# Four layers with routed experts: halves of the hidden rows treated later in a step, and half-groups' weights loaded from ScalarE's queue

## The chip, the cores and the metric

One core of a Trainium2 chip. The metric is the device time of one execution in microseconds (us), as the median of several runs. The profile describes one further execution of the same program. Engines are named as in the profile: PE is TensorE (PEld its weight loads), DVE is VectorE, ACT is ScalarE, POOL is GpSimd, SP is SyncE (SPq its queue of DMA issues).

## The reference, cut to what matters

64 sequences of 64 tokens with 256 features pass through four residual layers. The stage that the change touches is layer 0:

```
rw = softmax(cond_8);  w, sel = top_k(rw, 2)          # two of 8 experts per sequence
out  = sum over the two chosen: w * (gelu(x @ gate) * (x @ up)) @ down     # 256 -> 1024 -> 256
out += the same with the shared expert's weights
x = x + out
```

Layers 1 (a weight matrix mixed per sequence), 2 (low rank) and 3 (one expert of 8, silu) follow and are not touched.

## The kernel before, in words

The kernel is written by hand, engine by engine. Each engine has its own list of instructions, and counting semaphores order them. Layer 0 first does the shared expert for half of the sequences, then the chosen experts, then the shared expert for the other half, interleaved with layers 1 and 2. The chosen stage has NR0 = 68 steps `s`. Sixty steps treat a full group: two sequences (128 token rows) that chose the same expert. Eight treat a mixed group in two halves, in which the two sequences have different experts. The steps stand as two first steps, a loop of NMIXED0 = 4 rounds of BODY = 16 steps `k` each, and two last steps. In a round the mixed half groups are the steps k = 4 (half 0) and k = 12 (half 1) (`HALVES`).

Products are done in split precision: fp32 data are split into a high part (by ACT) and a low part (by DVE). The 1024 hidden features of a group come in two halves, `h` = 0 and 1. In step s:

- PE does up and gate of half 0 of group s (L771 to L773, or L792 for a mixed group), then the down product of half 0 of group s-2 (L860 to L863), then up and gate of half 1 of group s, then down of half 1 of group s-2.
- ACT does `gelu` (L1298) of each half, the high part of the x of the next group (L1292), and the high parts `hh` of the turned hidden rows of group s-1 (`hidden_hi_chosen`, L1312, L1314).
- DVE does `hidden` (gelu times up, L1832), its transposition within squares of 32 (L1840), the low part of x (L1805), the low parts `hl` of the turned hidden rows of group s-1 (`hidden_lo_chosen`, L1845, L1847), and the weighted sum of group s-2 (`add`, L1909 to L1916).
- The other part of the transposition goes through DRAM: SP writes the squares (`write_square`, L422) and reads them back in turned order (`read_hidT`, L429). ACT's `hh` waits for this read, DVE's `hl` for `hh`, and the down product for `hl`.
- SP also loads the x of group s+2 (`load_skill`), stores finished rows (`store_chosen`, L376), and loads the mixed groups' expert weights (`load_mixed0`, L384): six pieces of 512 KB per half, that is gate, up and down for each of two experts.
- POOL loads the weights of the next expert in pieces of 512 KB on its own queue (L612) and splits them (L617, L619) in what is called a turn here; there is one turn per expert.

The order of DVE's work is written out in `chosen_group`: hidden 0, squares 0, x of the next group, `hl` 0 of s-1, hidden 1, squares 1, add of s-2, `hl` 1 of s-1. ACT's order is gelu 0, x, `hh` 0, gelu 1, `hh` 1. `hidT[h]` is one buffer per half, so that a read of it may start only when the low part of the group before has been made of it. In the kernel before that follows from DVE's order.

Of the kernel before, what the change touches and what calls it, by code (L numbers as in the profile page):

```python
# [40 lines left out]
E = 8  # L41
# [6 lines left out]
NR0 = FULL0 + 2 * NMIXED0  # L48
# [5 lines left out]
S0, S1 = EARLY, EARLY + NR0  # L54
# [8 lines left out]
PIECE = 1024  # L63
# [13 lines left out]
BODY = NR0 // NMIXED0 - 1  # L77
HALVES = (4, 12)
# [8 lines left out]
def place_at(m, k):  # L87

    m, k = m + k // BODY, k % BODY
    past = sum(k > at for at in HALVES)  # L90
    stored = 7 * m + 1 + k // 2 - (k > HALVES[0]) if k % 2 == 0 else 8 * m + 1 + k // 2
    return Place(2 + (BODY - 2) * m + k - past, HALVES.index(k) if k in HALVES else None, m, stored)


def place(s):

    return place_at((s - 2) // BODY, (s - 2) % BODY)
# [6 lines left out]
def build(nc, x, xT, cond, condT, w0, w1, mask, b1, w2, b2, w3, b3, out):  # L104
# [5 lines left out]
    with ExitStack() as ctx:  # L110
# [179 lines left out]
        def table_values(engine, at, top):  # L290

            return nc.values_load_multi_w_load_instructions(
                at, engines=[engine.engine], min_val=0, max_val=top,
                skip_runtime_bounds_check_because="the routing bounds what the table holds")[1]
# [15 lines left out]
        def _(sp):  # L310
# [62 lines left out]
            def store_chosen(g, r, at):  # L373
                sp.wait_ge(acc_done, g + 1)
                f = at.full if at.half is None else FULL0 + at.mixed
                sp.dma_start(chosen_rows[bass.ds(f, 1)].rearrange("a p d -> (a p) d"), chosen_out[r])\  # L376
                    .then_inc(stored[r], 16)

            def load_mixed0(m, half, pieces, free):
                experts = table_values(sp, chosen_mixed0[0:1, bass.ds(2 * m, 2)], E)  # L380
                sp.wait_ge(acc_done, free)
                for k in pieces:
                    i, e = k // 2, experts[k % 2]
                    sp.dma_start(mixed0_w[k], w0[bass.ds(e, 1), :, (3 * half + i) * PIECE:(3 * half + i + 1) * PIECE]  # L384
                                 .rearrange("a p n -> p (a n)")).then_inc(mixed0_in[i], 16)

            def load_chosen(n, u, buffer, after=None):

                slots = [s for i in range(4)
# [11 lines left out]
            for n in range(0, WPIECES - 4, 4):  # L401
                g = WFIRST + n // 2 + 4
# [15 lines left out]
            def write_square(s, p, h, at):  # L418

                n = P if at.half is None else S  # L420
                sp.wait_ge(squared, 2 * s + h + 1)
                sp.dma_start(squares[p, h].rearrange("p (g x) -> p g x", g=4)[:, :, 0:n],  # L422
                             square[h][:, 0:4 * n].rearrange("p (g x) -> p g x", g=4)).then_inc(square_out[h], 16)

            def read_hidT(s, p, h, at):

                n = P if at.half is None else S
                sp.wait_ge(square_out[h], 16 * s + 16)
                sp.dma_start(hidT[h].rearrange("p (a x) -> p a x", a=4)[:, :, 0:n],  # L429
                             squares[p, h].rearrange("(a i) (g x) -> (i g) a x", a=4, g=4)[:, :, 0:n])\  # L430
                    .then_inc(hidT_in[h], 16)
# [8 lines left out]
            write_square(1, 1, 0, FIRST_TWO[1])  # L440
            read_hidT(0, 0, 1, FIRST_TWO[0])
            write_square(1, 1, 1, FIRST_TWO[1])
            read_hidT(1, 1, 0, FIRST_TWO[1])
            with sp.Fori(0, NMIXED0) as m:
                for k in range(BODY):
                    s, p = 2 + BODY * m + k, k % 2
                    at, before = place_at(m, k), place_at(m, k - 1)
                    load_skill(S0 + s + 2, p, place_at(m, k + 2))
                    write_square(s, p, 0, at)
                    read_hidT(s - 1, 1 - p, 1, before)  # L450
                    if k < 2:
                        load_mixed0(m, 0, ((0, 1, 2, 3), (4, 5))[k], S0 + BODY * m)
                    if k in (HALVES[0] + 3, HALVES[0] + 4):
                        load_mixed0(m, 1, ((0, 1, 2, 3), (4, 5))[k - HALVES[0] - 3], S0 + BODY * m + HALVES[0] + 3)
                    write_square(s, p, 1, at)
                    read_hidT(s, p, 0, at)
                    if place_at(m, k - 2).half != 0:
                        store_chosen(S0 + s - 2, p, place_at(m, k - 2))

            def load_late(t, ks=(0, 1)):  # L460
                for k in ks:
                    sp.wait_ge(xl_done, S1 + 2 * t + k - 1)
                    load_x(EARLY + 2 * t + k, k)
# [8 lines left out]
            write_square(NR0 - 2, 0, 0, LAST_TWO[0])  # L472
            read_hidT(NR0 - 3, 1, 1, place(NR0 - 3))
            write_square(NR0 - 2, 0, 1, LAST_TWO[0])
            read_hidT(NR0 - 2, 0, 0, LAST_TWO[0])
            store_chosen(S1 - 4, 0, place(NR0 - 4))
            load_late(0, (1,))
            write_square(NR0 - 1, 1, 0, LAST_TWO[1])
            read_hidT(NR0 - 2, 0, 1, LAST_TWO[0])
            write_square(NR0 - 1, 1, 1, LAST_TWO[1])  # L480
            read_hidT(NR0 - 1, 1, 0, LAST_TWO[1])
            store_chosen(S1 - 3, 1, place(NR0 - 3))
            sp.wait_ge(hl_done, 2 * S1 - 2)
            read_hidT(NR0 - 1, 1, 1, LAST_TWO[1])
            load_late(1)
# [790 lines left out]
        def _(act):  # L1276
# [7 lines left out]
            def split_x(g, p, free=None, xset=1, mixed=False):  # L1284

                act.wait_ge(xraw_in[p], 16 * (g - p) + 32)
                if free is not None:
                    act.wait_ge(up_done, free)
                if mixed:
                    act.activation(xm[:, 0:P], xraw[p][:, 0:P], ACT.Copy).then_inc(xh_done, 1)  # L1290
                    return
                act.activation(xh[xset][p], xraw[p], ACT.Copy).then_inc(xh_done, 1)  # L1292
# [7 lines left out]
            def hidden_hi(h, n2, first=False):  # L1300
# [3 lines left out]
                    act.wait_ge(down_done, n2 - 1)  # L1304
                act.activation(hh[h], turn_ps[h][:, :], ACT.Copy).then_inc(hh_done, 1)

            def hidden_hi_chosen(s, h, at):

                act.wait_ge(hidT_in[h], 16 * s + 16)
                act.wait_ge(down_done, 2 * (S0 + s) + h - 1)  # L1310
                if at.half is None:
                    act.activation(by_chunk(hh[h]), turned_hid(h), ACT.Copy).then_inc(hh_done, 1)  # L1312
                else:
                    act.activation(hm[h][:, 0:P].rearrange("p (a t) -> p a t", a=4), turned_mixed(h, 0), ACT.Copy)\  # L1314
                        .then_inc(hh_done, 1)
# [44 lines left out]
                    hidden_hi_shared((q - 1) % 2, 2 * g + q - 1)  # L1360
                    mix(2 * q + 1)

            def chosen_group(s, p, at, before_at, after_at):

                g, n = S0 + s, 512 if at.half is None else D
                gelu(0, 2 * g, n=n)
                if before_at is None:
                    hidden_hi_shared(1, 2 * g - 1)
                if after_at is None:
                    for k in range(2):  # L1370
                        split_x(g + 1 + k, k, xset=0)
                else:
                    split_x(g + 1, 1 - p, free=2 * g, mixed=after_at.half is not None)
                if before_at is not None:
                    hidden_hi_chosen(s - 1, 0, before_at)
                gelu(1, 2 * g + 1, n=n)
                if before_at is not None:
                    hidden_hi_chosen(s - 1, 1, before_at)

            def group(g, p, n=3, after=1, xset=1):  # L1380
                gelu(0, 2 * g, first=n < 1)
# [33 lines left out]
            chosen_group(1, 1, FIRST_TWO[1], FIRST_TWO[0], place(2))  # L1415
            with act.Fori(0, NMIXED0) as m:
                for k in range(BODY):
                    chosen_group(2 + BODY * m + k, k % 2, place_at(m, k), place_at(m, k - 1), place_at(m, k + 1))
            chosen_group(NR0 - 2, 0, LAST_TWO[0], place(NR0 - 3), LAST_TWO[1])
            chosen_group(NR0 - 1, 1, LAST_TWO[1], LAST_TWO[0], None)  # L1420

# [174 lines left out]
        def _(dve):  # L1596
# [322 lines left out]
            def chosen_group(s, p, at, before_at, after_at, add_at=None):  # L1919

                g = S0 + s
                hidden_chosen(s, 0, at)
                if before_at is None:
                    hidden_lo_shared(1, 2 * g - 1)
                hidden_squares(s, 0, at)
                if after_at is None:
                    for k in range(2):
                        split_x(g + 1 + k, k, xset=0)
                else:
                    split_x(g + 1, 1 - p, mixed=after_at.half is not None)  # L1930
                if before_at is not None:
                    hidden_lo_chosen(s - 1, 0, before_at)
                hidden_chosen(s, 1, at)
                hidden_squares(s, 1, at)
                if before_at is None:
                    add_pair(g - 2)
                    return
                if add_at is not None:
                    add(g - 2, p, add_at)
                hidden_lo_chosen(s - 1, 1, before_at)  # L1940
# [317 lines left out]
```

## Time and profile before

| | us |
|---|---|
| median of 3 runs | 1205.19 |
| the three runs | 1205.19, 1205.22, 1196.62 |
| the profiled execution, its own time | 1200.89 |
| its span, first to last instruction | 1199.3 |
| PE busy in the span | 1134.5 |

A busy PE means that a matmul was in flight. The chosen stage lies between about 190 and 795 us of the span. The steps of one engine can be followed in the timeline, where a row is start, duration, engine, line and operation, with the idle time before it and its releaser in brackets.

### The profile page before, as it was taken

To read this page: it belongs to the slowest core of one execution; us is meant where nothing else is said; L and a number is where in the kernel's file an instruction comes from. 1 tells how busy PE (TensorE), PEld (TensorE's weight loads), DVE (VectorE), ACT (ScalarE), POOL (GpSimd) and SP (SyncE) were. 2 spreads that over 40 slices of the span, in tenths; PEclk is the share of its full clock that TensorE was granted. 3 is DMA by queue.
4 is the path that set the end of the run, shared out by engine and by line. 5 is a ranking of instruction groups with operands and counts; after the bars stand their busy time and mean duration, and the time that the engine had idled before them with its cause. 6 is when DMAs were issued, how large, how long until landed. Compare 5 with 4: busy or idle time off the path is not lost.

```text
span 1199.3 us, 25044 instructions
## 1 busy us (share of the span) xinstructions
PE 1134.5 (95%) x6894; PEld 956.9 (80%) x6895; DVE 743.0 (62%) x1255; ACT 428.2 (36%) x845; POOL 471.4 (39%) x296
## 2 busy tenths in 40 slices
PE   8999998998989999798997999989999999899998
PEld 7999996776776777676876677779999999678876
DVE  6775667657658587485875768655555555444443
ACT  5356532232222232222322232323332222566664
POOL 3278588106327045081451836010000000888840
PEclk9999999999999999899998999999999999999999
DMA  7189868777777866768667786556655546577753
GB/s 227 48 258 327 290 191 286 212 225 217 205 237 209 262 181 205 248 191 268 175 204 248 218 272 202 170 159 172 160 150 138 139 128 246 150 239 243 215 170 90
DMA packets 257126, 245.07 MB, mean 204 GB/s; under 512 B 89216, under 2 KB 216448, under 8 KB 254976
## 3 DMA queue, kind: packets, MB, share of 16 engines
q1 hardware_dynamic: 243344, 193.95, 53.4%
q0 software_dynamic: 13680, 49.81, 13.8%
q8 instruction: 57, 0.93, 0.3%
q14 instruction: 45, 0.37, 0.1%
HBM read 176.59 MB, written 67.11 MB: 203 GB/s over the span
## 4 chain that ended last, share of the span: by engine, by line
PE 70%; DMA 11%; DVE 7%; issue 5%; SPq 4%; ACT 2%; POOL 1%; DVEq 0%; ACTq 0%; POOLq 0%
PE bank L771 11%; PE bank L772 10%; PE bank L773 10%; DMA routing<-squares 10%; PE bank L1208 6%; PE bank L861 6%; PE bank L1237 3%; PE bank L792 3%; PE bank L1049 3%; PE bank L912 2%; PE bank L860 2%; PE bank L914 2%; PE bank L913 2%; PE bank L1186 2%; DVE FS L1832 1%
## 5 line engine op out<-in xcount | busy, mean ns | idle before, releaser
L617 POOL TENSOR_TENSOR W<-raw,one 128x1024 fp32r<-128x1024 f32 x79 | 150.8, 1909 | 565.9 <-DVE acc L1912 282.5
L861 PE MATMUL bank<-W,RS 128*128 x480 | 186.8, 411 | 34.4 <-DVE RS L1845 34.1
L771 PE MATMUL bank<-W,RS 128*128 (+1 forms) x512 | 206.9, 404 | 11.5 <-DVE RS L1805 9.1
L1845 DVE TENSOR_TENSOR RS<-routing,RS 128x512 fp32r<-128x512 f32 x120 | 130.4, 1087 | 131.3 <-ACT RS L1312 130.9
L1312 ACT ACTIVATE RS<-routing 128x512 fp32r<-128x512 f32 x120 | 75.8, 632 | 369.3 <-DMA routing<-squares 340.0
L619 POOL TENSOR_TENSOR W<-raw,W 128x1024 fp32r<-128x1024 f32 x79 | 200.2, 2535 | 6.2
L772 PE MATMUL bank<-W,RS 128*128 (+1 forms) x512 | 202.3, 395 | 0.0
L773 PE MATMUL bank<-W,RS 128*128 (+1 forms) x512 | 201.4, 393 | 0.0
L861 PEld LDWEIGHTS bank<-W,RS 128*128 128x128 f32 x480 | 91.8, 191 | 64.4 <-issue 49.7
L1298 ACT ACTIVATE FS<-bank 128x512 f32<-128x512 f32 (+1 forms) x200 | 114.2, 571 | 71.9 <-PE bank L773 70.2
L771 PE MATMUL bank<-RS,W 128*128 128x256 f32 x448 | 129.7, 289 | 1.0 <-DVE RS L1805 1.0
L771 PEld LDWEIGHTS bank<-W,RS 128*128 128x128 f32 x512 | 98.1, 192 | 40.4 <-issue 21.0
L773 PE MATMUL bank<-RS,W 128*128 128x256 f32 x448 | 127.0, 284 | 0.0
L772 PE MATMUL bank<-RS,W 128*128 128x256 f32 x448 | 127.0, 283 | 0.0
L773 PEld LDWEIGHTS bank<-W,RS 128*128 128x128 f32 x512 | 97.4, 190 | 21.2
L772 PEld LDWEIGHTS bank<-W,RS 128*128 128x128 f32 x512 | 97.9, 191 | 19.8
L1832 DVE TENSOR_TENSOR FS<-bank,FS 128x512 f32<-128x512 f32 (+1 forms) x136 | 88.7, 652 | 36.2 <-PE bank L773 27.3
L860 PE MATMUL bank<-W,RS 128*128 x360 | 102.9, 286 | 0.0
L771 PEld LDWEIGHTS bank<-RS,W 128*128 128x128 f32 x448 | 86.2, 192 | 1.3 <-issue 1.2
L772 PEld LDWEIGHTS bank<-RS,W 128*128 128x128 f32 x448 | 86.2, 192 | 0.1
L773 PEld LDWEIGHTS bank<-RS,W 128*128 128x128 f32 x448 | 86.1, 192 | 0.0
L1208 PE MATMUL bank<-W,RS 128*128 x336 | 84.0, 399 | 0.4 <-issue 0.3
(236 smaller groups left out, 2046.9 us busy)
## 6 DMA issues: line engine op xcount, KB each, us to landing
raw<-in_w POOLq DMA_DIRECT2D x87, 512.0 KB, 4.9
acc<-in_w SPq DMA_DIRECT2D x70, 512.0 KB, 5.5
routing<-squares SPq DMA_DIRECT2D x120, 256.0 KB, 3.2
mixes<-acc SPq DMA_DIRECT2D x16, 1024.0 KB, 6.2
W<-mixes SPq DMA_DIRECT2D x16, 1024.0 KB, 6.1
squares<-X SPq DMA_DIRECT2D x60, 256.0 KB, 2.4
squares<-acc SPq DMA_DIRECT2D x60, 256.0 KB, 2.9
FS<-in_xT SPq DMA_DIRECT2D x200, 64.0 KB, 2.9
```

What stands on the lines that cost most here:

```text
L617: pool.tensor_tensor(hi, raw[:, k, :], ones_like(PIECE), ALU.mult).then_inc(done, 1)
L619: pool.tensor_tensor(lo, raw[:, k, :], hi.bitcast(F32), ALU.subtract).then_inc(done, 1)
L771: pe.matmul(ps, ah, bh, start=(i == 0), stop=False)
L772: pe.matmul(ps, ah, bl, start=False, stop=False)
L773: mm = pe.matmul(ps, al, bh, start=False, stop=(i == n - 1))
L860: pe.matmul(ps, chunk(hl[h], c), w2_[:, 0, :], start=False, stop=False)
L861: mm = pe.matmul(both, chunk(hh[h], c), w2_, start=(h == 0 and c == 0), stop=(h == 1 and c == 3))
L1208: mm = pe.matmul(ps[:, :], chunk(x, c), w, start=False, stop=(c == 1 and x is x3l), skip_group_check=True)
L1298: act.activation(gl[h][:, 0:n], gate_ps[h][:, 0:n], ACT.Gelu_apprx_tanh).then_inc(gelu_done, 1)
L1312: act.activation(by_chunk(hh[h]), turned_hid(h), ACT.Copy).then_inc(hh_done, 1)
L1832: TT(hid[h][:, 0:n], up_ps[h][:, 0:n], gl[h][:, 0:n], ALU.mult).then_inc(hid_done, 1)
L1845: TT(by_chunk(hl[h]), turned_hid(h), by_chunk(hh[h].bitcast(F32)), ALU.subtract).then_inc(hl_done, 1)
```

## The change

1. DVE: `hl` 0 of group s-1 moves behind hidden 1 and squares 1 of group s, and stands ahead of the add of s-2. In a step whose add belongs to a mixed half 0 it stands between hidden 1 and squares 1.
2. ACT: gelu 1 moves ahead of `hh` 0. The order is gelu 0, x, gelu 1, `hh` 0, `hh` 1.
3. SP: `read_hidT(s, 0)` moves behind `store_chosen(s-2)`. That store waits until the add of group s-2 is done, and this wait now also protects `hidT[0]`. In the first steps a wait for `hl` is added, and in the last two steps the stores move likewise.
4. `load_mixed0` moves from SP to ACT, behind gelu 1, and its pieces are spread. Half 0 has pieces 0 and 1 at k = 0, and pieces 2, 3, 4, 5 at k = 1, 2, 3, 4. Half 1 has the same at k = 7 and k = 8 to 11. Before, there were four pieces at k = 0 (7) and two at k = 1 (8).

```diff
@@ SP
-            def load_mixed0(m, half, pieces, free):
-                ...
             write_square(1, 1, 1, FIRST_TWO[1])
+            sp.wait_ge(hl_done, 2 * S0 + 1)
             read_hidT(1, 1, 0, FIRST_TWO[1])
             with sp.Fori(0, NMIXED0) as m:
                 for k in range(BODY):
...
                     read_hidT(s - 1, 1 - p, 1, before)
-                    if k < 2:
-                        load_mixed0(m, 0, ((0, 1, 2, 3), (4, 5))[k], S0 + BODY * m)
-                    if k in (HALVES[0] + 3, HALVES[0] + 4):
-                        load_mixed0(m, 1, ((0, 1, 2, 3), (4, 5))[k - HALVES[0] - 3], S0 + BODY * m + HALVES[0] + 3)
                     write_square(s, p, 1, at)
-                    read_hidT(s, p, 0, at)
                     if place_at(m, k - 2).half != 0:
                         store_chosen(S0 + s - 2, p, place_at(m, k - 2))
+                    read_hidT(s, p, 0, at)
@@ ACT
+            def load_mixed0(m, half, pieces, free):
+                experts = table_values(act, chosen_mixed0[0:1, bass.ds(2 * m, 2)], E)
+                act.wait_ge(acc_done, free)
+                for k in pieces:
+                    i, e = k // 2, experts[k % 2]
+                    act.dma_start(mixed0_w[k], ...).then_inc(mixed0_in[i], 16)
...
+                gelu(1, 2 * g + 1, n=n)
+                if mixed is not None:
+                    m, k = mixed
+                    if k <= HALVES[0]:
+                        load_mixed0(m, 0, ((0, 1), (2,), (3,), (4,), (5,))[k], S0 + BODY * m)
+                    elif HALVES[0] + 3 <= k < HALVES[0] + 8:
+                        load_mixed0(m, 1, ((0, 1), (2,), (3,), (4,), (5,))[k - HALVES[0] - 3],
+                                    S0 + BODY * m + HALVES[0] + 3)
                 if before_at is not None:
-                    hidden_hi_chosen(s - 1, 0, before_at)
-                gelu(1, 2 * g + 1, n=n)
-                if before_at is not None:
-                    hidden_hi_chosen(s - 1, 1, before_at)
+                    for h in range(2):
+                        hidden_hi_chosen(s - 1, h, before_at)
@@ DVE
-                if before_at is not None:
+                hidden_chosen(s, 1, at)
+                first = add_at is not None and add_at.half == 0
+                if first:
                     hidden_lo_chosen(s - 1, 0, before_at)
-                hidden_chosen(s, 1, at)
                 hidden_squares(s, 1, at)
...
+                if not first:
+                    hidden_lo_chosen(s - 1, 0, before_at)
                 if add_at is not None:
                     add(g - 2, p, add_at)
                 hidden_lo_chosen(s - 1, 1, before_at)
```

## Rows read from the trace of the kernel before

**Rows 1.** The page: busy time of each engine in the span.
```profile
PE 1134.5 (95%) x6894; PEld 956.9 (80%) x6895; DVE 743.0 (62%) x1255; ACT 428.2 (36%) x845; POOL 471.4 (39%) x296
```

**Rows 2.** PE's waits between 200 and 800 us: total, times, longest.
```profile
PE bank L861 <- DVE RS L1845: 33.7, 18, 5.9
PE bank L771 <- DVE RS L1805: 9.1, 8, 1.7
```

**Rows 3.** Timeline of PE, SP, ACT, 480 to 503 us, around one set of pieces.
```profile
480.07 0.39 PE L771 MATMUL bank<-W,RS 128*128 x1
...
480.85 1.90 SPq L384 DMA_DIRECT2D acc<-in_w  x4
...
483.98 0.49 PE L861 MATMUL bank<-W,RS 128*128 x1 [1.03 <-DVE RS L1845]
...
485.90 0.49 PE L771 MATMUL bank<-W,RS 128*128 x1 [0.25 <-issue]
...
492.98 0.63 ACT L1312 ACTIVATE RS<-routing 128x512 fp32r<-128x512 f32 x1 [9.17 <-DMA routing<-squares]
...
494.75 0.79 PE L861 MATMUL bank<-W,RS 128*128 x1 [5.85 <-DVE RS L1845]
...
497.47 0.63 PE L771 MATMUL bank<-W,RS 128*128 x1
...
502.89 0.40 PE L771 MATMUL bank<-W,RS 128*128 x1
```

**Rows 4.** The chain that ended last, 470 to 500 us: start, duration, what.
```profile
479.80 0.80 SPq L292
...
483.67 9.29 DMA routing<-squares
```

**Rows 5.** Windows: length, busy of PE, PEld, DVE, ACT, POOL, clock, DMA share, GB/s.
```profile
471.00:480.00 9.00, 9.00 (x46) 7.59 (x45) 6.22 (x12) 2.54 (x5) 0.00 (x0) 1.00 0.53 161
480.00:490.00 10.00, 7.62 (x34) 5.50 (x32) 2.31 (x4) 1.42 (x3) 0.00 (x0) 1.00 0.92 296
490.00:500.00 10.00, 5.25 (x14) 4.33 (x15) 5.08 (x9) 2.81 (x6) 0.00 (x0) 0.66 0.83 263
...
585.00:620.00 35.00, 34.34 (x180) 25.75 (x178) 29.29 (x35) 9.32 (x20) 29.93 (x18) 1.00 0.71 203
```

**Rows 6.** PE's timeline: first and last of the 18 stalls near sets of pieces.
```profile
200.47 0.49 PE L861 MATMUL bank<-W,RS 128*128 x1 [1.41 <-DVE RS L1845]
...
724.46 0.49 PE L771 MATMUL bank<-W,RS 128*128 x1 [1.05 <-DVE RS L1805]
```

**Rows 7.** Timeline of a step without pieces or turn, 422 to 431 us.
```profile
423.33 0.68 DVE L1832 TENSOR_TENSOR FS<-bank,FS 128x512 f32<-128x512 f32 x1
...
425.15 0.39 PE L861 MATMUL bank<-W,RS 128*128 x1
...
425.89 0.69 DVE L1845 TENSOR_TENSOR RS<-routing,RS 128x512 fp32r<-128x512 f32 x1 [0.73 <-ACT RS L1312]
...
426.08 0.43 SPq L429 DMA_DIRECT2D routing<-squares  x1
426.50 0.68 DVE L1832 TENSOR_TENSOR FS<-bank,FS 128x512 f32<-128x512 f32 x1
...
427.21 0.71 DVE L1840 STREAM_TRANSPOSE acc<-FS 128x512 f32<-128x512 f32 x1
...
429.28 0.39 PE L861 MATMUL bank<-W,RS 128*128 x1
...
429.83 0.69 DVE L1845 TENSOR_TENSOR RS<-routing,RS 128x512 fp32r<-128x512 f32 x1 [0.92 <-ACT RS L1312]
```

**Rows 8.** Timeline in a turn of POOL, 442 to 448 us.
```profile
442.88 0.54 SPq L429 DMA_DIRECT2D routing<-squares  x1
...
444.08 2.60 DVE L1845 TENSOR_TENSOR RS<-routing,RS 128x512 fp32r<-128x512 f32 x1 [0.92 <-ACT RS L1312]
...
447.01 0.31 ACT L1314 ACTIVATE acc<-routing 128x128 f32<-128x128 f32 x1 [2.17 <-DMA routing<-squares]
```

More of the change, by code:

```diff
@@ L377, in store_chosen @@
                     .then_inc(stored[r], 16)
-            def load_mixed0(m, half, pieces, free):
[L380 to L385, printed above, removed]
             def load_chosen(n, u, buffer, after=None):
@@ L474, in _ @@
             write_square(NR0 - 2, 0, 1, LAST_TWO[0])
+            load_late(0, (1,))
+            store_chosen(S1 - 4, 0, place(NR0 - 4))
             read_hidT(NR0 - 2, 0, 0, LAST_TWO[0])
-            store_chosen(S1 - 4, 0, place(NR0 - 4))
-            load_late(0, (1,))
             write_square(NR0 - 1, 1, 0, LAST_TWO[1])
@@ L480, in _ @@
             write_square(NR0 - 1, 1, 1, LAST_TWO[1])
+            store_chosen(S1 - 3, 1, place(NR0 - 3))
             read_hidT(NR0 - 1, 1, 0, LAST_TWO[1])
-            store_chosen(S1 - 3, 1, place(NR0 - 3))
             sp.wait_ge(hl_done, 2 * S1 - 2)
@@ L1305, in hidden_hi @@
                 act.activation(hh[h], turn_ps[h][:, :], ACT.Copy).then_inc(hh_done, 1)
+            def load_mixed0(m, half, pieces, free):
[3 more added lines that the diff above has]
+                    i, e = k // 2, experts[k % 2]
+                    act.dma_start(mixed0_w[k], w0[bass.ds(e, 1), :, (3 * half + i) * PIECE:(3 * half + i + 1) * PIECE]
+                                 .rearrange("a p n -> p (a n)")).then_inc(mixed0_in[i], 16)
             def hidden_hi_chosen(s, h, at):
@@ L1361, in pair_shared, with chosen_group @@
                     mix(2 * q + 1)
-            def chosen_group(s, p, at, before_at, after_at):
+            def chosen_group(s, p, at, before_at, after_at, mixed=None):
                 g, n = S0 + s, 512 if at.half is None else D
@@ L1417, in _ @@
                 for k in range(BODY):
-                    chosen_group(2 + BODY * m + k, k % 2, place_at(m, k), place_at(m, k - 1), place_at(m, k + 1))
+                    chosen_group(2 + BODY * m + k, k % 2, place_at(m, k), place_at(m, k - 1), place_at(m, k + 1),
+                                 (m, k))
             chosen_group(NR0 - 2, 0, LAST_TWO[0], place(NR0 - 3), LAST_TWO[1])
```

## The prediction

> **What bounds the kernel now.** I read the page first. PE is busy for 1134.5 of 1199.3 us [rows 1], so the core is nearly matmul-bound, and the most that can be won by better ordering is what PE loses. Then I read PE's waits in the chosen stage. They come to 33.7 us for the low part of the turned hidden rows, 9.1 us for the low part of x [rows 2], and about 2 us of small ones: 44.8 us together. The question is what makes `hl` late. A clean step shows that it need not be: up-and-down units on PE follow each other every 4.13 us (425.15 to 429.28, [rows 7]), so a full step takes 8.26 us, with no idle time.
>
> The timeline around a set of pieces shows the cause [rows 3, 4]. Four pieces of 512 KB are issued at 480.85 on SP's queue. The read of turned rows issued behind them at 483.67 lands only after 9.29 us. In the clean step the same read takes 3.1 us (issued 426.08, landed when ACT's `hh`, 0.63 us before `hl` at 429.83, could start [rows 7]). ACT waits 9.17 us, gelu 1 stands behind that wait, DVE waits for `hh`, and PE stops for 5.85 us. The same set had already stopped PE for 1.03 us at 483.98 and 0.25 us at 485.90. There are eight such sets (two halves in each of four rounds).
>
> Idle time is not the whole loss. The starts of up and gate at 480.07, 485.90, 497.47 and 502.89 are 5.83, 11.57 and 5.42 us apart against 4.13, which is 1.70 + 7.44 + 1.29 = 10.4 us lost for 7.13 us idle, a factor of 1.46. Part of the difference is matmuls that run slower behind the stop: the mean granted clock of 490 to 500 us is 0.66 [rows 5], so for part of that stretch TensorE had its lower level of 1.2 GHz. PE had been idle for 5.85 us before.
>
> I went through PE's timeline for the stalls within some 20 us behind a set. There are 18, the first at 200.47 and the last at 724.46 [rows 6], with 32.6 us idle: 5.3, 1.1, 3.9, 1.8, 7.1, 3.2, 7.2 and 3.1 us for the eight sets. Times 1.46 they cost 47.7 us. The other 12.2 us idle (some 18 us of loss) lie in turns of POOL, in which DVE's operations are stretched: an `hl` takes 2.60 us in place of 0.69 [rows 7, 8].
>
> **The change part by part.**
>
> *Pieces on ACT's queue, one per step.* What it removes from SP is 1.90 us of issue at k = 0 and the 0.80 us of register loads ahead of it [rows 3, 4]. What matters more is the burst. Four pieces delayed one read by 9.29 - 3.1 = 6.2 us, that is 1.5 us per piece (the other two pieces of the set, issued later, has no part in this). The critical loop in a step is hidden 0, squares 0, write, read, `hh` 1, `hl` 1, hidden 0 of the next step. It took 7.11 us in the clean step (423.33 to 430.44, where `hl` of 429.83 ends [rows 7]), against 8.26 us that PE needs, so it regains 1.15 us per step. If a piece still costs a read 1.5 us, a step with one piece has a loop of 8.6 us, 0.4 us too long, and the step with two has 10.2 us, 1.9 us too long. A set then builds up 1.9 + 4 x 0.4 = 3.5 us of lag. `hl` 1 has 2.9 us in hand (done 430.52, wanted 4.13 us behind 429.28, at 433.41), so 0.6 us of it reaches PE. Sets that fall into a turn of POOL have less in hand. I take 1.5 us per set, 12 us in all. The bounds are 0 and the whole lag with nothing in hand, 28 us.
>
> The trace shows no DMA issue and no such register load on ACT in this stage. By SP's rows a load costs 0.80 us and an issue about 0.48 us. That is 1.8 us of ACT at the step with two pieces and 1.3 us at the others, between gelu 1 and `hh` 0. It delays `hh` 0 and `hh` 1. ACT is busy 2.54 of 9 us in a clean stretch [rows 5], and `hh` 0 is now wanted only behind squares 1, so I take 0. The upper bound is that all of it reaches PE: 8 x (1.8 + 4 x 1.3) = 56 us. The lower bound is 0. The wait for the add count in front of the pieces asks for an add made a step earlier and is met. Behind it on ACT stand `hh` 0 and 1, and behind those DVE's `hl` and the down product. POOL's own loads keep their place on their own queue.
>
> *gelu 1 ahead of `hh` 0.* In the clean step `hh` 0 came from the read and delayed gelu 1, so that hidden 1 started at 426.50 though its matmuls had ended about 425.3. DVE waited 0.73 us there [rows 7]. The edit frees this time, and a late read of half 0 no longer holds up hidden 1 and the next write. On a clean step this is worth nothing, since PE doesn't wait. In turns of POOL it gives up to 0.73 us in each of about 30 steps (a turn is some 35 us [rows 5], 4.2 steps, seven or eight turns), an upper bound of 20 us.
>
> *`hl` 0 behind squares 1.* This is what the change costs. With time counted from the start of the down product of half 1 in step s (425.15 in the clean step), hidden 1 can start at about +0.25, squares 1 ends at +1.64, and `hl` 0 at +2.35. The down product of half 0 wants it at +4.13 [rows 7], less some 0.4 us between the end of `hl` and the start of PE (`hh` of 0.63 us from 492.98 and `hl` of 0.69 us end at 494.3, PE starts at 494.75 [rows 3]). So 1.3 us are in hand, where before `hl` 0 ended at 426.58, with 2.7 - 0.4 = 2.3 us in hand. In a clean step that costs nothing. Where POOL holds `hl` 0 for 2.60 us [rows 8], it ends 0.6 us too late. Over 30 steps that would be 18 us, if each were hit in full. DVE is busy 29.29 of 35 us in such a turn, against 6.22 of 9 us outside [rows 5]. That is 0.84 against 0.69, or 1.2 us more per step over five operations that can be hit, so a typical step isn't hit in full. I take 5 us lost here and 2 us won by the gelu edit: net 3 us. The bounds are 18 lost and 20 won.
>
> *The read of half 0 behind the store.* It is now issued after the add of s-2, which needs two operations behind `hl` 0: about +3.4, and the store and its own issue bring it to +4.0, against +3.3 before. It lands at +7.1, and `hh` 0 ends at +7.8. It is wanted at 8.26 + 1.64 = +9.9. Nothing is late until a read takes over 5 us. Price 0. SP's x load behind it moves by the same 0.7 us at most, and is not wanted for another step. The added wait at the start and the moved stores at the end count once each, 0 to 1.4 us, taken as 0.
>
> *The sum.* -47.7 + 12 + 3 = -33 us, against the profiled execution's own 1200.89 us: 1168 us. The median of the runs is 4.3 us above that execution, and the lowest run is 4.3 us below it, so I leave the forecast there: **1168 us**, a gain of some 3%. A part of the gain may be lost outside the stage, though I see no row for it: PE is the bound behind it too.
>
> **The rivals.**
>
> *The queue makes no difference.* In the trace the read is late by what lies in front of it, and the share of the DMA engines rises from 0.53 to 0.92 when a set runs [rows 5]. If bytes alone count and nothing is in hand at most sets, each set costs its whole lag of 3.5 us, 28 us in all. The time is then 1201 - 47.7 + 28 = **1181 us**, or 1184 with the 3 us above. For it speaks that some sets fall into turns, where a read already takes 4.1 us (442.88 to 447.01 [rows 8]). Against it speaks that the share has room: a clean step has 0.53, and one piece a step adds little over 0.1. The Trainium skill (DMA: Bandwidth & Descriptors, Issuing engines are not separate DMA queues) states this as a rule: DMAs of several issuing engines share the same 16 engines, and another issuer saves only issue time. By that rule this rival would hold, and the gain would come from the spreading alone. The same page (Queues, rings and completion order) has each DMA engine take turns between the queues' rings, packet by packet, by which a short read would pass a long piece of another queue; the trace has no case on the hardware queues to tell.
>
> *DVE gains too.* The stalls in turns shrink as well, since DVE no longer waits in mid-step: 18 us of loss fall by half, and the pieces cost only the 0.6 us of an undisturbed set, 5 us in all. Then 1201 - 47.7 + 5 - 9 = **1149 us**. For it speaks the 0.73 us wait in each step; against it the smaller reserve of `hl` 0.
>
> *`hl` 0 is late in most steps: slower.* The place is DVE's `hl` 0 behind squares 1, and behind it the add, the store and the read of the next group. It decides from the point at which a read of half 0 takes longer than 5.0 + 1.3 = 6.3 us in a step without a turn, or 4.4 us in one where POOL stretches `hl` 0 by 1.9 us. Reads take 3.1 us clean and 4.1 us in a turn. With a piece beside it, at 1.5 us, a read in a turn takes 5.6 us and is over. If some 55 of 68 steps have a turn or a piece and lose 1.5 us each, that is 82 us: 1201 - 47.7 + 82 = **1235 us**. Against it speaks that pieces and turns seldom meet, and that 3.1 + 1.5 = 4.6 us is under 6.3.
>
> *Nothing moves.* The stalls come from DVE's order and not from the reads, or new ones take their place one for one: about 1200 us. The 9.29 us in the chain [rows 4] speak against it.
>
> **How the numbers follow.** Chances: forecast (1158 to 1176) 0.52, queue rival (1176 to 1189) 0.18, DVE gains 0.14, nothing 0.07, slower 0.09. The range should leave out the slower case and the "nothing" case: 1147 to 1191. It holds the bound of 28 us for the pieces plus several us of the `hl` bound, and nearly the whole case of DVE's gain on the other side. About 12 us (1%) is what a measurement of this kernel can tell from no change. Faster by over 1%: 0.52 + 0.18 + 0.14 = 0.84, less 0.02 for the queue rival's tail: 0.82. Within 1%: 0.07 + 0.02 and a share of the mild end of the slower case: 0.10. Slower: 0.08.
>
> **What the profile after should show.** PE's wait for L1845 falls from 33.7 us to 5 to 15 us, with no single stall above 3 us near the pieces. The reads behind a piece land within 5 us. ACT's longest wait for a read falls from 9.2 to some 5 us. A third DMA queue appears with the 48 pieces. In a clean step gelu 1 runs right behind its matmuls, and DVE has `hl` 0, add and `hl` 1 in a row, with a wait only before the last. The stalls in turns remain, some by the new place of `hl` 0. The granted clock no longer dips in windows like 490 to 500 us. The prediction is wrong if the reads take 6 us or more beside single pieces, if ACT's register loads take several us, or if DVE's order makes PE wait in clean steps.

## The result, and the profile after

The changed kernel takes 1193.32 us (median of 20 runs, 1186.63 to 1199.33), the kernel before 1202.26 us (median of 20 runs, 1196.62 to 1206.87). The ratio is 0.9928, with a 95% interval of 0.9907 to 0.9949. That is a gain of 0.7% or some 9 us, where 33 us were forecast. The profiled execution took 1193.86 us, its span is 1192.3 us.

PE's waits in the chosen stage, 200 to 800 us (line, releaser: total, times, longest), which answer to [rows 2]:

```profile
PE bank L850 <- DVE RS L1849: 22.4, 20, 1.9
PE bank L760 <- DVE RS L1809: 7.9, 8, 1.4
PE bank L760 <- DVE FS L1836: 7.0, 6, 1.5
```

The long stops are gone: the longest wait for the low part of the hidden rows is 1.9 us, against 5.9 us. But the total of the stage is still some 40 us against 44.8 us. Many short stops have come in place of few long ones, and PE now also waits for hidden 0 (L1836).

The page's queues, and the transposition's DMAs with their medians (count, size, us to landing):

```profile
q1 hardware_dynamic: 236432, 168.78, 46.8%
...
q10 hardware_dynamic: 6912, 25.17, 7.2%
...
routing<-squares SPq DMA_DIRECT2D x120, 256.0 KB, 3.9
...
squares<-X SPq DMA_DIRECT2D x60, 256.0 KB, 3.3
squares<-acc SPq DMA_DIRECT2D x60, 256.0 KB, 4.0
```

q10 is ACT's queue with the 48 pieces (25 MB). In the kernel before, the page has 3.2, 2.4 and 2.9 us for the three last rows. All three are now longer in the median over the whole execution.

The timeline of a step with one piece, outside POOL's turns, which answers to [rows 3] and [rows 7]:

```profile
413.53 0.34 ACTq L1301 DMA_DIRECT2D acc<-in_w  x1
...
413.95 0.33 SPq L414 DMA_DIRECT2D squares<-X  x1
...
414.32 0.43 SPq L421 DMA_DIRECT2D routing<-squares  x1
...
415.63 0.65 DVE L1849 TENSOR_TENSOR RS<-routing,RS 128x512 fp32r<-128x512 f32 x1
...
416.20 0.47 DVE L1916 TENSOR_SCALAR acc<-bank,weight 128x256 f32<-128x256 f32 x1
...
417.47 0.35 SPq L376 DMA_DIRECT2D chosen_rows<-acc  x1
...
419.69 0.38 SPq L421 DMA_DIRECT2D routing<-squares  x1
...
420.45 0.63 ACT L1309 ACTIVATE RS<-routing 128x512 fp32r<-128x512 f32 x1 [5.75 <-DMA routing<-squares]
```

Two things are to be seen. The piece is issued at 413.53, just ahead of the write of half 0 (413.95) and the read of half 1 (414.32). That read lands only when ACT can start at 420.45, 6.1 us later, against 3.1 us in [rows 7]. The read of half 0 could have gone at 417.82, behind the store, but goes at 419.69: it waits for the write of 413.95, which took about 5.7 us. So a piece holds up both halves of the round trip. DVE meanwhile does what the change asks: `hl` 0 at 415.63 right behind squares 1, then the add.

The windows which answer to [rows 5] (length, busy of PE, PEld, DVE, ACT, POOL, clock, DMA share, GB/s):

```profile
396.00:432.00 36.00, 35.58 (x171) 29.27 (x170) 21.89 (x40) 11.00 (x22) 0.00 (x0) 1.00 0.76 222
480.00:490.00 10.00, 8.60 (x41) 6.72 (x40) 5.08 (x9) 2.43 (x5) 0.00 (x0) 1.00 0.80 248
```

The DMA share is 0.76 over a whole set, where before it stood at 0.92 behind a burst and at 0.53 without. In these windows the granted clock is full. It still dips once in the stage, in a turn of POOL (here a window of 10 us with the same columns):

```profile
650.00:660.00 10.00, 7.48 (x35) 5.10 (x34) 7.79 (x8) 2.11 (x5) 8.88 (x6) 0.76 0.93 268
```

Before, there were five such dips (near 210, 350, 493, 562 and 643 us). Over the span the clock is 0.994 against 0.989.

The idle time of PE has also moved. I count as a turn each stretch in which POOL's splits follow each other, and 2 us behind it. Between 195 and 785 us PE idled 20.7 us in turns and 24.0 us outside them in the kernel before. Now it idles 32.6 us in turns and 8.0 us outside.

### The profile page after: what moved, and what is told of

Same layout as the page of the kernel before. It is cut to its first block, busy times and chain, and to the rows that moved or that the text cites. A ratio compares the mean times of both kernels' runs of the same rounds, so it can differ in the third digit from the quotient of the medians.

```text
span 1192.3 us, 25071 instructions
## 1 busy us (share of the span) xinstructions
PE 1130.8 (95%) x6894; PEld 951.8 (80%) x6895; DVE 743.8 (62%) x1255; ACT 430.0 (36%) x845; POOL 468.0 (39%) x296
## 4 chain that ended last, share of the span: by engine, by line
PE 60%; DMA 16%; DVE 8%; issue 7%; SPq 5%; ACT 2%; POOL 1%; ACTq 1%; DVEq 0%; POOLq 0%
DMA routing<-squares 14%; PE bank L760 10%; PE bank L761 9%; PE bank L762 9%; PE bank L1197 7%; PE bank L1226 3%; PE bank L850 3%; PE bank L1038 2%; DVE FS L1836 2%; PE bank L901 2%; DVE RS L1809 2%; PE bank L1175 2%; PE bank L903 2%; PE bank L902 2%; DVE X L1844 1%
## 5 line engine op out<-in xcount | busy, mean ns | idle before, releaser
L850 PE MATMUL bank<-W,RS 128*128 x480 | 183.5, 404 | 23.4 <-DVE RS L1849 22.9
L761 PE MATMUL bank<-W,RS 128*128 (+1 forms) x512 | 200.9, 392 | 0.0
L608 POOL TENSOR_TENSOR W<-raw,W 128x1024 fp32r<-128x1024 f32 x79 | 196.9, 2492 | 6.2
L760 PEld LDWEIGHTS bank<-W,RS 128*128 128x128 f32 x512 | 96.7, 189 | 50.8 <-issue 30.8
L850 PEld LDWEIGHTS bank<-W,RS 128*128 128x128 f32 x480 | 90.4, 188 | 52.7 <-issue 38.7
L761 PE MATMUL bank<-RS,W 128*128 128x256 f32 x448 | 127.1, 284 | 0.0
L1836 DVE TENSOR_TENSOR FS<-bank,FS 128x512 f32<-128x512 f32 (+1 forms) x136 | 88.6, 652 | 47.7 <-ACT FS L1287 32.7
L762 PEld LDWEIGHTS bank<-W,RS 128*128 128x128 f32 x512 | 96.6, 189 | 20.5
L761 PEld LDWEIGHTS bank<-W,RS 128*128 128x128 f32 x512 | 96.7, 189 | 18.8
L849 PE MATMUL bank<-W,RS 128*128 x360 | 101.7, 282 | 0.0
L761 PEld LDWEIGHTS bank<-RS,W 128*128 128x128 f32 x448 | 86.3, 193 | 0.1
L1197 PE MATMUL bank<-W,RS 128*128 x336 | 84.1, 399 | 0.4 <-issue 0.3
```

The source lines that it names most:

```text
L608: pool.tensor_tensor(lo, raw[:, k, :], hi.bitcast(F32), ALU.subtract).then_inc(done, 1)
L760: pe.matmul(ps, ah, bh, start=(i == 0), stop=False)
L761: pe.matmul(ps, ah, bl, start=False, stop=False)
L762: mm = pe.matmul(ps, al, bh, start=False, stop=(i == n - 1))
L849: pe.matmul(ps, chunk(hl[h], c), w2_[:, 0, :], start=False, stop=False)
L850: mm = pe.matmul(both, chunk(hh[h], c), w2_, start=(h == 0 and c == 0), stop=(h == 1 and c == 3))
```

## The experiments

All ratios are to the kernel before, run on the same chip (medians of 1199.6 to 1203.1 us there). In all of them the layout of the work is as told above; only what is named is changed.

**The two parts of the change, each alone.** First the pieces on ACT's queue in the old order:

```diff
  ACT:  gelu 0, x, hh 0, gelu 1,
+       load_mixed0 (the change's schedule),
        hh 1
  SP:  -load_mixed0;   DVE and the reads as before
```

> The order of before on all engines; only the loading of the mixed groups' pieces moves to ACT's queue, one per step (two in the first). Theory N (neighbours): a piece on a queue of its own slows every write and read of squares beside it by about 3 us, as the read issued at 414.32 in the changed kernel took 6.1 us and the write at 413.95 5.7 us; it does so in 40 steps, where the burst did it in 16. Then this kernel shows most of what the change won and lost: 1185 to 1200 us, with ratio 0.985 to 1.00, reads of 5 to 6 us beside pieces. Theory O (order): the burst was worth the 33 us forecast and hl 0 behind squares 1 gave 24 us back in POOL's turns. Then this kernel is the fastest, some 1165 to 1175 us, ratio 0.97 to 0.975.

Measured: 1195.96 us, 0.991 (0.987 to 0.995). This is the changed kernel's own gain. Theory O falls here: the order gave nothing back.

Then the order alone, with the bursts on SP's queue:

```diff
  the changed kernel's DVE, ACT and SP order
-       ACT: load_mixed0, spread
+       SP:  load_mixed0, pieces 0 to 3 at k = 0 (7), 4 and 5 at k = 1 (8)
```

> The new order on DVE, ACT and SP, with the pieces in bursts of four and two on SP's queue as before. Theory N: the stalls behind the bursts stay, a little smaller because gelu 1 and hidden 1 no longer wait for the late read: 1190 to 1203 us. Theory O: the bursts cost as before and the smaller reserve of hl 0 comes on top: 1212 to 1230 us, ratio 1.01 to 1.02, PE waits for the low part of the hidden rows in POOL's turns at the mixed groups.

Measured: 1205.98 us, 1.0024 (1.0006 to 1.0043), 3 us above theory N's range of 1190 to 1203 us and 6 us below theory O's. With a burst in front, the new order doesn't help.

**The same spreading on SP's queue.**

```diff
  the changed kernel
-       ACT, behind gelu 1: load_mixed0, spread
+       SP, between read_hidT(s - 1, 1) and write_square(s, 1): load_mixed0, same schedule
```

> As the changed kernel, but the pieces, one per step as there, are issued by SP behind the read of half 1. This tells the queue from the spreading. If the queue matters by letting short reads pass (the ring rule of the notes), this is slower than the changed kernel by some 10 us: about 1203 us. If a queue of its own is what hurts, because write and read ahead of a piece are now slowed by it too, this is faster: 1175 to 1185 us. If only bytes count (another issuer saves only issue time), it is equal within 4 us: 1190 to 1197 us.

Measured: 1181.26 us, 0.9821 (0.9786 to 0.9856). It is faster than the changed kernel by 12 us, with intervals apart. The same pieces in the same steps cost less when SP issues them behind the read. Two things differ from the changed kernel: the queue, and the moment of the issue within the step. DMAs by window show where (here 388 to 424 us, and in the changed kernel 396 to 432 us, both with six pieces and no turn):

```profile
acc<-in_w SPq DMA_DIRECT2D x6, 512.0 KB, 4.9
routing<-squares SPq DMA_DIRECT2D x8, 256.0 KB, 3.4
squares<-acc SPq DMA_DIRECT2D x5, 256.0 KB, 4.5
squares<-X SPq DMA_DIRECT2D x4, 256.0 KB, 2.5
```

```profile
acc<-in_w ACTq DMA_DIRECT2D x6, 512.0 KB, 4.5
routing<-squares SPq DMA_DIRECT2D x9, 256.0 KB, 4.3
squares<-X SPq DMA_DIRECT2D x5, 256.0 KB, 4.5
squares<-acc SPq DMA_DIRECT2D x4, 256.0 KB, 5.2
```

With SP's queue (the first block) the write of half 0 (from X) takes 2.5 us and a read 3.4 us, as without pieces. With ACT's queue they take 4.5 and 4.3 us. Only the write of half 1, which follows the piece on SP's queue, pays in both. A read of half 1 and the piece behind it, in the kernel with SP's queue:

```profile
403.27 0.43 SPq L429 DMA_DIRECT2D routing<-squares  x1
...
404.72 0.34 SPq L384 DMA_DIRECT2D acc<-in_w  x1
...
406.22 0.63 ACT L1314 ACTIVATE RS<-routing 128x512 fp32r<-128x512 f32 x1 [1.28 <-DMA routing<-squares]
```

The read lands within 2.95 us, although a piece is issued while it runs.

The old order with the same spreading on SP's queue:

> Old order on all engines; only the pieces are spread, on SP's queue, as in the run with the new order that took 1181 us. If spreading alone does it, 1178 to 1185 us. If the new order pays once the burst is gone (gelu 1 and hidden 1 no longer wait for a late read of half 0), this is slower than 1181: 1188 to 1196 us. Theory O: faster than 1181, 1168 to 1175 us.

Measured: 1187.06 us, 0.9846 (0.981 to 0.9882). The new order may be worth 3 to 6 us once the burst is gone. The intervals overlap, so that isn't settled.

**Without the bytes.**

```diff
-  dma_start(mixed0_w[k],          w0[e, :, at:at + PIECE])
+  dma_start(mixed0_w[k][:, 0:64], w0[e, :, at:at + 64])
```

> The changed kernel, but each of the 48 pieces loads 64 of its 1024 columns, so that the mixed groups compute with incomplete weights: all instructions and waits stay, the bytes go. Theory N: what is left of the pieces' cost goes, 25 to 40 us: 1155 to 1168 us. Theory O: only the forecast's 12 us go, about 1181 us, and the stalls at mixed groups in POOL's turns stay at their size (some 3 us each).

> The kernel before, but each piece loads 64 of its 1024 columns: incomplete weights in the mixed groups. It says what the bursts cost in all, and, beside the changed kernel with small pieces (1168.8 us), what the new order does by itself. Forecast of the prediction: the pieces cost 47.7 us, so 1155 us, and the new order would cost 3 us by the prediction and 14 us by these two. Theory N: the pieces cost less than 47.7 us because lag from POOL's turns was counted with them; 1165 to 1175 us, the order then being worth between -5 and +5 us. Theory O: 1145 to 1155 us.

> The control for ACT's own share: the new order with small pieces (64 of 1024 columns, incomplete weights) issued by SP, spread as in the run of 1181 us. Beside the same with the issue on ACT (1168.8 us) it says what the register loads and issues on ACT cost without the bytes. If nothing, as I took it: 1166 to 1171 us, and the 12 us between ACT's and SP's queue are the bytes' doing. If ACT's in-order queue is what costs: 1157 to 1162 us.

Each piece brings 64 of its 1024 columns, so the mixed groups compute with incomplete weights. All instructions and waits stay.

| small pieces | us | ratio (interval) | the same with full pieces | cost of the bytes |
|---|---|---|---|---|
| e4, new order, ACT's queue | 1168.79 | 0.9708 (0.9679 to 0.9736) | 0.9928 | 0.0220, 26 us |
| e5, old order, bursts on SP's queue | 1167.45 | 0.9701 (0.9678 to 0.9725) | 1 | 0.0299, 36 us |
| e15, new order, SP's queue, spread | 1165.62 | 0.9678 (0.9645 to 0.9710) | 0.9821 | 0.0143, 17 us |

The three kernels without bytes lie within 0.3% of each other. So the new order by itself shows no harm here (e5 against e4 and e15), and ACT's own register loads and issues cost some 3 us (e4 against e15), with intervals that overlap. The bytes make the difference: 36 us in bursts, 26 us spread as in the change, 17 us spread behind the read of half 1 by SP.

PE's waits in the old kernel without the bytes, 195 to 785 us:

```profile
PE bank L861 <- DVE RS L1845: 16.3, 18, 1.9
PE bank L771 <- DVE RS L1805: 7.8, 7, 1.4
...
PE bank L792 <- DVE acc L1803: 1.9, 3, 0.9
PE bank L771 <- issue: 0.8, 3, 0.3
PE bank L861 <- issue: 0.3, 1, 0.3
```

These are 27.1 us that no piece's bytes can have caused, and 25.0 us of them lie in turns of POOL. (The wait of 4.3 us that is left out belongs to the next stage.) Of the 44.8 us idle before, 17.7 us are then the pieces', not 32.6 us. This is one execution of each kernel, and this one took 1175.81 us, the slowest of its six (median 1167.45 us), so the split is rough. The clock's part of the cost would show in PE's busy time, 1125.4 us here against 1134.5 us [rows 1]. But the changed kernel without the bytes has 1132.9 us, so that single executions don't settle this part.

The changed kernel without the bytes (e4) idles 14.6 us in turns and 5.5 us outside, against 32.6 and 8.0 us with them. (This profiled execution too is the slowest of its six, 1175.31 us.) So most of the idle time that the spread bytes add lies in turns of POOL.

**The moment of the issue, and the queue.** On ACT's queue the pieces were also issued at another moment than on SP's. Three kernels were to tell these apart.

```diff
e9_act_late:   ACT: gelu 1, hh 0, hh 1, +load_mixed0
e12_act_mid:   ACT: gelu 1, hh 0, +load_mixed0, hh 1
e10_sp_early:  SP: load_skill, +load_mixed0, write_square(s, 0), read_hidT(s - 1, 1), write_square(s, 1)
```

> As the changed kernel, with pieces on ACT's queue, but issued at the end of ACT's step, behind hh 1 of s-1, when the read of half 1 has landed. It tells the moment from the queue. Moment theory: what hurts is that a piece is issued beside the write of half 0 and the read of half 1 of the same step, which are in the shortest loop; moved behind them it costs as on SP's queue: 1178 to 1186 us. Queue theory: a queue of its own slows the short transfers whenever it is issued: 1190 to 1197 us as the changed kernel.

Measured: 1189.63 us, 0.9918 (0.9892 to 0.9944). The ratio lies within the interval of the changed kernel, as the queue theory said. But this kernel doesn't refute the moment theory, since the piece only moved to another short transfer. In its trace, 35 of the 48 pieces are issued between 2.6 us ahead of a read of half 0 and 1 us behind it, and none so near a read of half 1. The median read of half 1 falls to 3.6 us (changed kernel 4.4 us), and that of half 0 rises to 4.2 us (3.6 us).

> The new order with the pieces spread on SP's queue, but issued ahead of the write of half 0, so that this write and the read of half 1 stand behind each piece. Moment theory: as the changed kernel or worse, since here the write and the read wait for the whole piece: 1192 to 1205 us. Queue theory: the short transfers keep to one queue, so 1181 us as with the pieces behind the read.

Measured: 1219.07 us, 1.0158 (1.0118 to 1.0197). On SP's queue the moment decides: ahead of the write and the read instead of behind them, the same pieces cost 0.034 of the time, some 40 us, more. The queue theory, as I had put it, falls for this one.

> As the changed kernel, pieces on ACT's queue, issued between hh 0 and hh 1, that is 1 to 2 us behind the start of the read of half 1, as on SP's queue in the run of 1181 us, but on the other queue. If only the moment counts: 1179 to 1185 us. If a queue of its own lets a piece slow a read that was issued before it: reads of half 1 of 5 us or more beside pieces, against 2.9 to 3.5 us on SP's queue, and 1188 to 1196 us.

Measured: 1197.47 us, 0.9989 (0.9962 to 1.0016), slower than I had expected. One of its reads with a piece beside it:

```profile
494.29 0.43 SPq L421 DMA_DIRECT2D routing<-squares  x1
...
494.58 0.34 ACTq L1301 DMA_DIRECT2D acc<-in_w  x1
...
499.26 0.63 ACT L1309 ACTIVATE RS<-routing 128x512 fp32r<-128x512 f32 x1 [4.73 <-DMA routing<-squares]
```

The read was issued 0.29 us before the piece and still took 5.0 us. In another step of the same kernel the piece came 1.38 us behind the read:

```profile
406.31 0.43 SPq L421 DMA_DIRECT2D routing<-squares  x1
...
407.69 0.34 ACTq L1301 DMA_DIRECT2D acc<-in_w  x1
...
409.39 0.63 ACT L1309 ACTIVATE RS<-routing 128x512 fp32r<-128x512 f32 x1 [2.16 <-DMA routing<-squares]
```

This read landed within 3.1 us, like the one on SP's queue above (2.95 us, with the piece 1.45 us behind). So the edit did not do what it was meant to do. Only 12 of the 48 pieces came 1 to 2.6 us behind a read of half 1, where SP's issue puts all 48, 12 came within 1 us behind it and 17 up to 2.6 us ahead of it.

The traces can be sorted by this distance instead. The table has the median time to landing outside POOL's turns, for transfers of 256 KB with one piece issued from 4 us ahead to 2.5 us behind, and the number of cases. ACT's queue: the changed kernel, e1, e9 and e12. SP's queue: e3, e6, e8, e10, e11 and e13.

| issue of the piece | read of half 1, ACT's queue | read of half 1, SP's queue | write of half 0, ACT's queue | write of half 0, SP's queue |
|---|---|---|---|---|
| 0 to 1.3 us ahead | 5.20 (12) | 5.43 (11) | 4.91 (8) | 4.84 (10) |
| 0 to 1 us behind | 4.95 (9) | no case | 2.40 (18) | no case |
| 1 to 2.5 us behind | 3.05 (10) | 3.17 (105) | 2.38 (12) | 2.37 (114) |
| no piece near | 3.19 (59) | 3.31 (53) | 2.40 (62) | 2.42 (69) |

Where both queues have cases, they agree within 0.25 us. In these rows what counts is how far the piece stands ahead of the transfer or behind it. That a queue of its own makes a piece dearer isn't shown. Not explained by these rows is the size of the difference between whole kernels: e9 and e12 are 0.010 and 0.017 of the time (some 12 and 20 us) slower than e3, although the reads of half 1 in e9 take nearly as long as in e3.

**Bursts on ACT's queue.** The changed kernel with the schedule of before (four pieces, then two):

> The changed kernel with the pieces on ACT's queue but in the bursts of before (four and two). By theory N a burst on a queue of its own shares the engines with the reads instead of standing ahead of them: fewer steps are disturbed (16 instead of 40), each by up to 6 us. 1190 to 1205 us. If spreading is what counts and the queue nothing: as the order alone on SP's queue, 1206 us.

Measured: 1203.13 us, 1.0009 (0.9989 to 1.0029). So spreading is what gives the changed kernel its gain. A burst costs about as much on either queue (1.0009 here, 1.0024 on SP's), with intervals that overlap.

**The number of pieces per step.**

```diff
e8:   pieces 0, 1, 2, 3, 4, 5 at k = 0 to 5 and k = 7 to 12
e11:  half 0 as the change; half 1: 0 to 5 at k = 6 to 11
e13:  half 0: 0 at k = 15 of the round before, 1 to 5 at k = 0 to 4; half 1 as in e11
(all: new order, SP's queue, behind read_hidT(s - 1, 1); e13 loads a 49th piece in the last round, unused)
```

> Candidate: the new order, pieces on SP's queue, exactly one in each of six steps, so that no step has two. The step with two cost about 1.8 to 2.5 us of excess in the changed kernel, eight times. If that holds on SP's queue: 1181 - 8 = 1173 us; if the step with two is covered there: 1181 us.

Measured: 1198.44 us, 0.9963 (0.9936 to 0.9989), a miss. PE's waits in it:

```profile
PE bank L793 <- DMA acc<-in_w: 23.2, 8, 5.0
PE bank L862 <- DVE RS L1846: 7.6, 10, 1.9
```

PE waits 23.2 us for the fourth piece, which it needs at k = 4 (12) and which was issued one step before. All other stops of the stage come to 10.8 us. The two next kernels start each set one step earlier.

> Candidate: the new order, pieces on SP's queue behind the read of half 1; half 0 as in the run of 1181 us, half 1 with exactly one piece per step from k = 6, a step earlier, so that its fourth piece lands before PE wants it. The run with six even steps from k = 0 and 7 had PE wait 23.2 us for pieces and only 12 us for the rest, against 29 us with two in the first step. Half of the 17 us difference for half 1: about 1173 us. If the double step isn't what made the difference: 1181 us.

Measured: 1178.51 us, 0.9813 (0.9781 to 0.9845).

> Candidate: new order, SP's queue, exactly one piece in each of six steps for both halves, each set starting one step earlier (k = 15 of the round before and k = 6), so that the fourth piece lands in time. The double steps of half 0 still cost in the run of 1178.5 us: 4 x 1 us gained, 1172 to 1177 us. If the double step is covered: 1178 us.

Measured: 1177.12 us, 0.9821 (0.9784 to 0.9858). Both beat the kernel before and the changed one (0.9928). Between them and the spreading of the change on SP's queue (0.9821) there is no difference that these runs can tell. e11 missed its forecast of 1173 us and lies between its two cases, and e13's 1177.12 us lies between the two of its own, which are 1 us apart. The two are 0.011 of the time, some 13 us, faster than the changed kernel.

**POOL's turns.** What is left without bytes:

```diff
  POOL, from the third turn on (on top of e4's small pieces):
-   tensor_tensor(lo,          raw[:, k, :],    hi,          subtract)
+   tensor_tensor(lo[:, 0:64], raw[:, k, 0:64], hi[:, 0:64], subtract)
```

> The changed kernel with small pieces (1168.8 us), and POOL's second operation of each piece's split, the low part of the weights, on 64 of 1024 columns from the third turn on: low parts of the weights incomplete. It takes away over half of POOL's time beside DVE. If the stalls that stay without piece bytes (about 20 us idle) come from DVE's operations stretched by POOL, as the prediction says of 18 us: 1152 to 1160 us, with the mean of an hl falling from 1.07 to some 0.8 us. If they are a matter of order: 1168 us.

The low parts of POOL's split are thus incomplete. Measured: 1160.12 us, 0.967 (0.9635 to 0.9706). The median is just outside the range of 1152 to 1160 us. It is 9 us below that of e4, but on another chip; by the ratios it is some 5 us, and the intervals overlap. PE's waits, 195 to 785 us, and the mean of an `hl` (fourth number from the left in the last row, ns):

```profile
PE bank L851 <- POOL W L609: 5.5, 4, 2.6
PE bank L851 <- DVE RS L1850: 4.8, 8, 1.2
...
L1850 DVE TENSOR_TENSOR RS<-routing,RS 128x512 fp32r<-128x512 f32 x120 | 109.6, 913 | 80.8 <-ACT RS L1310 80.6
```

In e4 the same wait is 14.9 us and the mean 1201 ns. (The 1.07 us of the expectation is about the mean with full pieces, 1.09 us.) So about 10 us of stops came from DVE's operations stretched beside POOL's, and over half of that is given back to a new wait, for POOL's own split (5.5 and 0.8 us). That the time fell is not clear of the noise, and the waits are those of one execution each.

## Why the prediction was wrong

The forecast was -47.7 + 12 + 3 = -33 us. The runs have -36 (bursts, e5), +26 (the same bytes spread on ACT's queue, e4), and some 1 us for order and issue together (e4 against e5): -9 us as measured. Two terms were mis-sized.

- **"They cost 47.7 us": the bursts cost 36 us.** I gave every stall within 20 us behind a set to the set, and scaled it by a factor from the worst one. The kernel without the bytes still idles for 27.1 us in the stage, 25.0 us of it in POOL's turns. I had left 12.2 us to the turns, where the trace of before has 20.7 us in them: sets often fall into turns, and I counted those stalls for the pieces. The factor of 1.46 fits: the two executions are 25.1 us apart for 17.7 us idle, 1.42. A stall near a cause isn't a stall by that cause.
- **"I take 1.5 us per set, 12 us in all": 26 us.** This is the step that failed. The term was worked out for a clean step: 3.5 us of lag per set, of which 2.9 us are in hand, and a little more taken for sets in turns. For a set clear of the turns (396 to 432 us) this came out. The reads of half 1 with a single piece just ahead took 4.3 to 6.1 us there (6.6 us with two), where my loop had 4.6 us. But the starts of hidden 0 (394.99, 404.79, 412.39, 421.73, 429.24 and 438.57 us) are 9.8, 7.6, 9.3, 7.5 and 9.3 us apart: every second step catches up. That is 2.3 us of lag against 3.5 us, and PE idled 0.4 us in this window against my 0.6 us. (In the set of 537 to 573 us, which starts as a turn ends, it idled 2.1 us.) What was wrong is the price of the sets in turns. PE idles 32.6 us in turns with the pieces, 14.6 us without their bytes, and 2.5 us more outside. So 18 of these 20.5 us of added idle time lie where I had put 0.9 us per set. Why a turn leaves so little in hand is argued only: an `hl` takes 2.60 us there in place of 0.69 us [rows 7, 8], and in the changed kernel `hl` 0 stands late in the step as well.
- **"A short read would pass a long piece of another queue".** I left this for the trace after, and priced the pieces as if it could only help. It doesn't help: with a piece up to 1.3 us ahead of it, a read of half 1 took 5.20 us with the piece on ACT's queue and 5.43 us with both on SP's. The Trainium skill (DMA: Bandwidth & Descriptors, Issuing engines are not separate DMA queues) says that another issuing engine saves only issue time. These rows agree. The same page (Queues, rings and completion order) has the DMA engines take turns between queues packet by packet. With this the 5.0 us of a read that was issued before the piece agrees; no run here shows the packets. The 12 us between ACT's and SP's issue of the same pieces go with the moment of the issue in these rows; no run holds the moment fixed and changes the queue alone.
- **The 9.29 us read, the eight sets, and the granted clock** were read rightly. The long stops vanished, and the clock rose from 0.989 to 0.994, with one dip left where there were five.
- **`hl` 0 behind squares 1** ran at +1.62 us against the +1.64 us worked out, and its price of 3 us lost is of the right size at most: the order alone lost 3 us with bursts (e2), and may have won 3 us without (e3 against e6, e15 against e5).
- **The read behind the store, "price 0"**, was incomplete. It is not the store that delays it but the write of its own half, which a piece slows. Its cost is in the 26 us.
- **ACT's issues, taken as 0** (bound 56 us): some 3 us, if anything (e4 against e15).
- **The rivals.** "The queue makes no difference" (1181 to 1184 us) was nearest in time. Its 28 us for the pieces are close to the 26 us measured, and no row contradicts its title. But it had every set pay its whole lag, and the set clear of the turns paid almost nothing, so this nearness is in part luck. "DVE gains too" and "`hl` 0 is late" didn't happen.
- **What the profile should have shown:** no stall above 3 us near the pieces and a third queue came as said, and the clock all but once. PE's wait for the low part (5 to 15 us foreseen, 22.4 us found), the reads (within 5 us foreseen, up to 8.3 us found) and ACT's longest wait (5 us foreseen, 7.1 us found) did not, and I had named reads of 6 us as what would make the prediction wrong.

## What to carry to other kernels

Spread bulk loads that share the DMA engines with a short round trip, and issue each of them right behind the round trip's most urgent transfer, here 1 to 2.5 us behind its issue. There they delay only what comes later. The engine that issues the urgent transfer can keep this order; another engine issues when its own work lets it, and in e12 only 12 of 48 loads came where they were meant to. Price what a delay costs in the steps that have the least in hand, not in a clean one: here these were the steps in POOL's turns. Start each set early enough that its last urgent piece lands a step before it is wanted. Before a cost is put down to bytes, run the kernel with the bytes taken out: it costs one run and would have corrected the largest term here.

## What the runs showed of the hardware that was not expected

- A read of 256 KB issued 0.29 us before a load of 512 KB on another queue took 5.0 us. With a load 1.38 us behind it on another queue it took 3.1 us, and 1.45 us behind it on its own queue 2.95 us. With a load up to 1.3 us ahead of it the median was 5.20 us on another queue and 5.43 us on the same.
- On one queue the place of the load decided over some 40 us: ratio 0.9821 with the pieces behind the read, 1.0158 with them ahead of the write and the read.
- Cutting POOL's subtraction from 1024 to 64 columns shortened the mean `hl` from 1201 to 913 ns, and PE's wait for it from 14.9 to 4.8 us. But PE then waited 6.3 us for POOL itself (5.5 us as shown and 0.8 us at L761).
